# Phase 1 of a three-layer graph kernel computes its exponentials transposed, with the row maxima brought across by one product

## What is computed

```
u = einsum('bid,bjd->bij', h, h) / sqrt(D)
a = softmax(u, axis=-1)
delta = a * adj
attn = delta / (sum(delta, axis=-1) + 1e-10)
ctx = (attn * upper) @ (h @ wl.T + bl) + diag(attn) * (h @ ws.T + bs) + (attn * lower) @ (h @ wr.T + br)
o = relu(layernorm(ctx) * g + beta)
```

## Time and profile before

| | us |
|---|---|
| median of 3 runs (1248.78 to 1248.87) | 1248.86 |
| profiled execution | 1248.56 |
| its span | 1246.8 |

### The profile page before, as it was taken

One profiled execution on the slowest core, in us unless ns is written; L12 is line 12 of the kernel. 1 busy time (PEld: TensorE's weight loads), 2 busy tenths in 40 slices (PEclk: granted clock), 3 DMA queues, 4 the chain that ended last, 5 costly groups with the idle time before them and its releaser, 6 DMA issues.

```text
span 1246.8 us, 27521 instructions
## 1 busy us (share of the span) xinstructions
PE 1228.9 (99%) x7258; PEld 1216.1 (98%) x7258; DVE 1065.0 (85%) x3057; ACT 823.4 (66%) x2047; POOL 335.3 (27%) x438
## 2 busy tenths in 40 slices
PE   8899999999999999999999999999999999999997
PEld 6899999999999999999999999999999999999997
DVE  6888888888887788888888888999999999999986
ACT  5676767676767666666666666676666666666663
POOL 2322222222222221221212222252323232323221
PEclk9899999999999999999999999999999999999999
DMA  5423232323234333233333323432232323332331
GB/s 176 132 83 118 82 118 82 118 82 118 82 105 122 106 108 106 88 94 98 95 105 94 91 95 95 156 109 77 98 102 98 102 98 101 99 101 99 100 97 45
DMA packets 112899, 126.91 MB, mean 102 GB/s; under 512 B 11104, under 2 KB 100192, under 8 KB 112864
## 3 DMA queue, kind: packets, MB, share of 16 engines
q1 hardware_dynamic: 112864, 126.50, 32.4%
HBM read 76.91 MB, written 49.55 MB: 101 GB/s over the span
## 4 chain that ended last, share of the span: by engine, by line
PE 95%; DVE 2%; issue 2%; ACT 1%; DMA 0%; SPq 0%; POOLq 0%; POOL 0%; DVEq 0%; ACTq 0%
PE right_bank L438 23%; PE left_bank L438 23%; PE context_bank L438 23%; PE context_bank L477 16%; PE score_bank L410 5%; PE score_bank L418 1%; PE edge_bank L430 1%; DVE weight L781 0%; DVE context L826 0%; PE right_bank L501 0%; DVE turned L716 0%; ACT nodes L534 0%; PE left_bank L501 0%; DMA nodes<-squares 0%; PE context_bank L501 0%
## 5 line engine op out<-in xcount | busy, mean ns | idle before, releaser
L438 PE MATMUL left_bank<-weight,node_t 128*128 128x384 f32 x1728 | 350.1, 345 | 0.4 <-DVE weight L781 0.3
L438 PE MATMUL context_bank<-weight,node_t 128*128 128x384 f32 x1728 | 332.4, 337 | 1.9 <-DVE weight L781 1.9
L438 PE MATMUL right_bank<-weight,node_t 128*128 128x384 f32 x1728 | 333.4, 337 | 0.4 <-ACT right_bank L581 0.4
L587 ACT ACTIVATE side_parts<-right_bank 128x384 fp32r<-128x384 f32 x192 | 94.4, 492 | 325.1 <-PE context_bank L477 325.1
L438 PEld LDWEIGHTS left_bank<-weight,node_t 128*128 128x128 f32 x1728 | 304.5, 189 | 4.7 <-issue 1.6
L438 PEld LDWEIGHTS context_bank<-weight,node_t 128*128 128x128 f32 x1728 | 303.6, 189 | 2.4 <-issue 2.2
L438 PEld LDWEIGHTS right_bank<-weight,node_t 128*128 128x128 f32 x1728 | 298.8, 188 | 0.6 <-issue 0.6
L477 PE MATMUL context_bank<-side_parts,attn_t 128*128 128x386 f32 x1152 | 241.7, 345 | 5.6 <-issue 5.0
L477 PEld LDWEIGHTS context_bank<-side_parts,attn_t 128*128 128x128 f32 x1152 | 199.8, 190 | 8.0 <-issue 7.0
L599 ACT ACTIVATE context_bank<-context_bank,diag 128x386 f32<-128x386 f32 x192 | 106.1, 553 | 59.2 <-PE context_bank L438 58.1
L716 DVE STREAM_TRANSPOSE turned<-nodes 128x768 f32<-128x768 f32 x94 | 92.0, 978 | 54.6 <-ACT nodes L534 44.0
(11 more groups left out here) (70 smaller groups left out, 1535.5 us busy)
## 6 DMA issues: line engine op xcount, KB each, us to landing
squares<-turned SPq DMA_DIRECT2D x94, 384.0 KB, 2.7
nodes<-squares SPq DMA_DIRECT2D x376, 96.0 KB, 2.2
rows<-x SPq DMA_DIRECT2D x64, 384.0 KB, 3.6
out<-rows SPq DMA_DIRECT2D x31, 384.0 KB, 2.6
adj_in<-adj SPq DMA_DIRECT2D x96, 64.0 KB, 1.9
piece<-weights SPq DMA_DIRECT2D x18, 192.0 KB, 2.5
rows<-weights SPq DMA_DIRECT2D x3, 576.0 KB, 7.7
vector_rows<-vectors SPq DMA_DIRECT2D x3, 384.0 KB, 8.1
```

The source lines that it names most:

```text
L438: mm = nc.tensor.matmul(bank[:, 0:D], node_t[:, s.parity, k, c, a], weight[:, s.phase % 2, w, c, b], start=False, stop=(c, a) == (CH - 1, ...
L587: nc.scalar.activation(side_parts[:, side, HI, 0:D], side_bank[side][k][:, 0:D], ACT.Copy).then_inc(side_hi[side], 1)
```

## The change

In phase 1 too the exponentials are now taken of the transposed scores. For a transposed row the maximum to subtract belongs to the free axis. VectorE puts the row maxima on a diagonal (`max_diag`: identity times maximum, 128 elements a partition), TensorE multiplies it with `same_graph` (ones in the two 64x64 diagonal blocks), which gives every partition of a graph the maxima of all its rows (`max_rows`, in `edge_bank`), and VectorE subtracts those. The row sums still need the untransposed form: ScalarE takes them from an exponential of the unshifted scores with the row's maximum as a bias (`totals`), into a copy that nobody reads (`score_copy`). The edge blocks are placed as in the bounded phases, the transposes and the second adjacency go.

```diff
+            def spread_max(s):
+
+                pe.wait_ge(max_placed, s.n + 1 - PAIRS)
+                nc.tensor.matmul(edge_bank[:, 0:2 * NODES], same_graph[:, :], max_diag[:, :, :].rearrange("p k i -> p (k i)"),
+                                 start=True, stop=True).then_inc(max_spread, 1)
+
+            def project(s, k, w, bank, done, within=None):
                 for c in range(CH):
+                    if c == CH - 1 and within is not None:
+                        within()
...
-                        if edges and c < 2 and a == HI:
-                            transpose_edges(s, c, b)
...
-                project_side(s, 1, LEFT)
+                project_side(s, 1, LEFT, within=(lambda: spread_max(nxt)) if nxt.exists() and not nxt.bounded else None)
...
+            def totals(s):
+                act.wait_ge(max_bias_done, s.n + 1 - PAIRS)
+                act.wait_ge(den_done, s.tile(0) - 2)
+                for k in range(2):
+                    nc.scalar.activation(score_copy[:, k], score[:, k], ACT.Exp, bias=max_bias[:, k:k + 1], scale=SCALE,
+                                         accum_out=total[:, s.parity, k:k + 1]).then_inc(total_done, 1)
+
             def exponentials(s):
-                if s.bounded:
-                    act.wait_ge(score_summed, 2 * s.n + 2)
-                else:
+                if not s.bounded:
                     act.wait_ge(shift_done, s.n + 1 - PAIRS)
+                    nc.scalar.activation(score[:, :, :], score[:, :, :], ACT.Exp, scale=SCALE).then_inc(exp_done, 2)
+                    return
...
             def split_edges(s):
-                    act.wait_ge(edges_moved, s.n + 1 - PAIRS)
-                    blocks = edge_bank[:, :]
+                act.wait_ge(blocks_placed, s.n + 1)
...
+            def place_max(s):
+
+                dve.wait_ge(max_done, s.n + 1 - PAIRS)
+                nc.vector.tensor_tensor(max_diag[:, :, :], tri[:, 4:5, :].to_broadcast([P, 2, NODES]),
+                                        row_max[:, :].bitcast(F32).unsqueeze(2).to_broadcast([P, 2, NODES]), ALU.mult).then_inc(max_placed, 1)
+                nc.vector.scalar_tensor_tensor(max_bias[:, :], row_max[:, :].bitcast(F32), 2 * SCALE, minus_half[:, :],
+                                               ALU.mult, ALU.mult).then_inc(max_bias_done, 1)
+
             def shift_scores(s):
-                dve.wait_ge(max_done, s.n + 1 - PAIRS)
-                nc.vector.tensor_tensor(score[:, :, :], score[:, :, :],
-                                        row_max[:, :].unsqueeze(2).to_broadcast([P, 2, NODES]),
-                                        ALU.subtract).then_inc(shift_done, 1)
+                dve.wait_ge(max_spread, s.n + 1 - PAIRS)
+                dve.wait_ge(total_done, 2 * (s.n + 1 - PAIRS))
+                nc.vector.tensor_tensor(score[:, :, :], score[:, :, :], max_rows, ALU.subtract).then_inc(shift_done, 1)
```

More of the change, by code:

```diff
@@ L189, in adj_gnn_program @@
         first_bank = [edge_bank, score_bank]
+        max_rows = edge_bank[:, 0:2 * NODES].rearrange("p (k i) -> p k i", k=2)
+        score_copy = cross[:, :, 0:NODES]
         scores4 = score_bank[:, :].rearrange("p (k a j) -> p k a j", k=2, a=2)
@@ L451, in weights_split, with project_side @@
                         pe.wait_ge(piece_lo, (s.phase - 1) * PIECES + (w + 1) * CH)
-            def project_side(s, k, side, edges=False):
+            def project_side(s, k, side, within=None):
                 pe.wait_ge(node_hi, s.n + 1)
@@ L485, in body @@
                     weigh(prev, 1)
-                project_side(s, 0, LEFT, edges=not s.bounded)
+                project_side(s, 0, LEFT)
                 if isinstance(s.n, int) and s.n == 0:
@@ L911, in body @@
                     input_shift(fourth)
+                if nxt.exists() and not nxt.bounded:
+                    shift_scores(nxt)
                 if prev.exists() and prev.phase > 0:
@@ L914, in body @@
                 centre(s, 0)
+                if nxt.exists() and not nxt.bounded:
+                    mask_edges(nxt)
                 split_side(s, 1, LEFT)
```

64 lines of the change are left out of this document (30 added, 34 removed).

## The result

| | us |
|---|---|
| before, median of 4 runs (1247.57 to 1248.87) | 1248.82 |
| after, median of 4 runs (1238.69 to 1239.96) | 1239.14 |
| ratio | 0.9925 [0.9913, 0.9937] |
| after, profiled execution | 1238.95 |
| its span | 1237.2 |

The changed kernel was run five times more later on, beside other kernels: 1239.11 us, ratio 0.9925 [0.9912, 0.9939]. The granted clock of TensorE was 0.994 of its full speed in the profiled execution before and in the one after.

A forecast was written before the change was run, and what follows sets the result against it. TensorE, busy 99% of the span, was taken as the bound. Steady steps -9.3, first product and memsets +0.2, end of phase 1 +4.35 gave -4.7: 1244.1 us against 1248.86, range 1241.2 to 1251.6.

The forecast's parts named there:

- The transposes: TensorE, phase 1: removing the four transposes of L430 saves 0.475 us in each of 32 steps.
- 27 steps: Phase 1's steps at 12.94 us become 12.60, TensorE still setting them: -9.3 us in all.
- The spread product: TensorE, left projection: one added 128x128 product per step costs 0.13 us and waits for nothing.
- VectorE's chain in the middle: Phase 1's steady step: later mask, own edges 0.47, longer node split; VectorE needs 12.4 us, under TensorE's 12.60.
- Rival (a): VectorE sets every step a little, at 12.75; the end costs 4.6; time 1248.5 us; chance 0.23.
- rival (b): GpSimd's own-edge product takes 0.81, step 12.8 to 12.85; time 1251.7 us; chance 0.15 with worse cases.
- Rival (d): The product stalls the left projection and costs the transposes' 0.475; time 1253 us; within the 0.15 for slower.
- ScalarE: Gains an exponential over 128 elements, 0.3 us; the self scale behind it stays covered by 0.4 us.
- The first step: The product falls in phase 0's last step; with the memsets, +0.2 us.
- The end: Phase 1's last steps, VectorE without air: 1.35 us in each of three, 0.3 in the one before; +4.35 us.
- Rival (c): Locks at the end cost 0.2, not 0.8, and the diagonal does not wait: end 1.6, time 1241.4 us; chance 0.15.
- The four memsets: Four small memsets at the program's start cost 0.1 us.

The follow-up runs named there:

- piece last: Changed kernel with GpSimd's second weight-piece split of phase 1 moved behind the three edge placings: 1237.55 us, ratio 0.9911 to the kernel before.
- three moves: Changed kernel, phase 1: mask ahead of centring, GpSimd's second piece behind the placings, ScalarE's second piece rounding ahead of the exponentials: 1236.36 us, ratio 0.9905.
- both moves: Changed kernel, phase 1: mask ahead of the centring and GpSimd's second piece split behind the placings: 1237.72 us, ratio 0.9912.

## Why the prediction was wrong

**The transposes, right in the middle.** 0.475 a step: the run without them gives 12.47. The sum used it in 27 steps only. Without them the first step and the end are shorter too, by 0.48 and 1.0 us, and both were put at nothing.

**The spread product, right.** 0.13 taken, 0.12 measured: the neighbouring pair's row gave its price to within 0.01.

**VectorE's chain in the middle, right.** Own edges 0.47, the diagonal's wait 0.19, the node split 1.84, and the step is TensorE's at 12.59 where 12.60 was forecast. Rival (a) would have needed a middle above 12.65 and rival (b) own edges of 0.81; neither is there. Against (b) the prediction named the left split as what the own edges would meet; phase 0's 0.47 at 411.70 meets no instruction of VectorE (the left split ends at 411.61), but the own edges of the changed kernel, at 612.92, do stand beside the left split (612.67 to 613.22) and take 0.47. The bias, counted with up to 0.16 of duration, takes 0.15 (at 608.72). Rival (d) is out too: the product waits for nothing. ScalarE was covered as the prediction counted: the exponential over 128 elements takes 0.31 (0.3 taken), the scale starts at 599.57 and ends at 600.11, the weighing at 600.71. Not seen was that an exponential with a bias from SBUF and a sum takes 0.34, where the exponential with a sum but no such bias takes 0.25; it cost nothing.

**The first step, wrong by 0.75.** The 27 steps gave -9.2 where -9.3 was forecast; but the step from 419.34 lasts 13.14 before and 12.59 after. The sum had +0.2 there, for the first product and the memsets, where the row gave -0.55. Of this, 0.48 is the transposes' (12.66 without them) and the product adds 0.12 again, so some 0.2 stays open. The score sum after the one at 419.34 (it stands at 432.48) could have been read.

**The end, wrong by 3.3 us, the step that failed.** The term of +4.35 measured +1.0. The prediction wrote: "Here VectorE has no air, and all that it gains it passes on", and added bias, shift, wait and a longer node split, 1.35 a step. The additions were right in kind, and the wait was even under-sized (0.84 at 804.26, and not 0.1 to 0.2). But it moved an instruction out of a place without asking what that place had cost. The mask took 0.58 and `in_shift` 0.87 there, beside GpSimd's pieces, and both were in the trace of before; 0.9 of the 1.7 came back that way and 0.34 through a wait for ScalarE that vanished. The steady step's durations were used for steps in which they do not hold. And VectorE was not alone there: the removed transposes give 1.0 us in the end steps, 0.28 of it in the last, for which the sum had no term and which went from 13.35 to 13.06. Rival (c), with 1.6 for the end, was the nearest, but by a mechanism that isn't there: locks small and no waiting.

**The start, 0.9 us not forecast.** No row on the loop's entry was read, since the change does not touch it; from the first score sum to phase 1 it is 1.1 us less, since the adjacency load at the loop's entry lands earlier, and why it does is open. The four memsets, put at 0.1 without a row, take 0.11 each and make TensorE's first product start at 2.01 instead of 1.53; what of that 0.48 reaches the end of the program is lost in the 1.4 us by which the traces differ at the first score sum.

So the mechanism of the gain was right and the size of the end term was wrong; 3.3 + 0.75 + 0.9, less 0.1 for the 27 steps, is 4.9, the difference between the two sums.

## What to carry to other kernels

When an instruction moves, price both places: what it will meet, and what it meets today. Where an instruction takes longer beside another engine's (a lock), compare its duration here with the same instruction's elsewhere (0.58 against 0.28, 0.87 against 0.13); the excess is what a move gives back. Take a trace of the kernel again before explaining a microsecond of its start: here two of the same kernel differ by 0.5 us at the first score sum. An end or start of a phase is not the steady step with a few things added: sum its own rows, and read the first and last pitches one by one. A wait whose releaser is called "issue" may be a transfer: add issue time and landing time of the loads that the instruction reads.

## What was not expected of the hardware

Of the node split and the weight piece now one and now the other is the longer, and it turned a gain round. With the split begun 0.47 us ahead they took 1.32 and 1.74 us (piece last), with the split 0.43 ahead 1.28 and 1.74 (three moves), and 1.82 and 1.01 where both begin at 803.87 (both moves). Against 0.94 to 0.96 with no instruction of GpSimd ahead, the split takes 1.84 behind the start of the edge blocks (613.62 and 613.34); what holds it, no run shows. An instruction with two elements a partition was held as well: `in_shift`, begun at 811.89, ends with GpSimd's second piece (812.76 and 812.74) and takes 0.87 instead of 0.13.

The landing of one 64 KB load behind two of 384 KB differs by 1 us between programs that issue the same loads (4.2 in three profiles against 3.1 to 3.4 in nine).
